# The order of transposed scores and look-ahead scores in the second and third pair of an attention step

## What is computed

```python
x = x + tanh(g_xattn[0]) * xattn(layernorm(x), ctx)
fused = layernorm(x) @ (Wa * col_scale)            # Q, K, V; col_scale from w_std, w_rec
scores = einsum('bhtd,bhsd->bhts', Qf, Kf) / sqrt(D)
scores = where(causal, scores, -max)
attn = softmax(scores); out = attn @ V
x = x + tanh(g_ffn[0]) * (out @ Wp)
```

## Time and profile before

| | |
|---|---|
| median of 3 runs | 578.65 us |
| the profiled execution | 577.93 us |
| its span in the trace | 576.2 us |
| PE busy | 482.2 us, 84% |
| DVE busy | 343.2 us, 60% |
| ACT busy | 262.6 us, 46% |
| POOL busy | 193.2 us, 34% |
| mean granted TensorE clock | 0.953 of full speed |

### The profile page before, as it was taken

How to read it: one execution, slowest core, us unless ns; L and a number is a source line. 1 busy time by engine, 2 the same in 40 slices (tenths; PEclk the granted TensorE clock), 3 DMA queues, 4 the chain that set the end, 5 groups by cost and what they waited for, 6 DMA issues and landing times.

```text
span 576.2 us, 8459 instructions
## 1 busy us (share of the span) xinstructions
PE 482.2 (84%) x2408; PEld 346.9 (60%) x2408; DVE 343.2 (60%) x970; ACT 262.6 (46%) x575; POOL 193.2 (34%) x288
## 2 busy tenths in 40 slices
PE   0036887887998999898798999898798999999977
PEld 0024765555776768665575768665576667666646
DVE  4779647579675353479776235568866116546522
ACT  0856333666544322556554322446565423434540
POOL 4665829137322252126422243124622100212210
PEclk9999999998897999798898999898899899999999
DMA  7202064332400243332400144422300134234001
GB/s 248 117 1 73 4 193 97 97 89 67 118 1 2 61 101 116 120 82 51 132 0 1 41 100 114 128 61 60 84 0 1 28 88 101 66 88 110 20 18 74
DMA packets 28022, 42.55 MB, mean 74 GB/s; under 512 B 8272, under 2 KB 8528, under 8 KB 27984
## 3 DMA queue, kind: packets, MB, share of 16 engines
q1 hardware_dynamic: 26448, 41.97, 26.2%
q10 hardware_dynamic: 1536, 0.14, 0.2%
HBM read 12.59 MB, written 4.19 MB: 29 GB/s over the span
## 4 chain that ended last, share of the span: by engine, by line
PE 57%; DVE 20%; ACT 11%; issue 6%; DMA 2%; ACTq 1%; SPq 1%; POOL 1%; DVEq 0%; POOLq 0%
PE pv_bank L631 10%; PE mm_bank L509 10%; PE mm_bank L510 9%; PE mm_bank L511 9%; ACT work L883 4%; DVE max_bank L1103 4%; PE max_bank L600 4%; PE exp_bank L617 3%; PE mm_bank L661 3%; PE mm_bank L659 3%; PE mm_bank L660 3%; PE turn_bank L517 2%; ACT tile_buf L822 2%; DVE x_amax L1056 2%; DMA col_root<-in_L_ffn_w_rec 1%
## 5 line engine op out<-in xcount | busy, mean ns | idle before, releaser
L1103 DVE CUSTOM_DVE_ANT_0 max_bank<-max_bank,causal 128x512 f32<-128x512 f32 (+3 forms) x256 | 119.1, 516 | 37.3 <-PE max_bank L600 34.5
L406 POOL TENSOR_SCALAR_AFFINE_SELECT work<-work 128x384 f32<-128x384 f32 x64 | 34.2, 534 | 270.0 <-ACT work L883 270.0
L883 ACT ACTIVATE work<-exp_bank 128x512 f32<-128x512 f32 (+1 forms) x192 | 91.1, 523 | 3.2 <-PE exp_bank L617 2.7
L617 PE MATMUL exp_bank<-q_stack,k_stack 97*128 97x512 f32 (+3 forms) x256 | 73.8, 371 | 7.8 <-ACT work L883 4.9
L631 PE MATMUL pv_bank<-work,v_aug 128*33 128x256 f32 (+3 forms) x512 | 75.1, 435 | 0.0
L600 PE MATMUL max_bank<-k_stack,q_stack 96*128 96x512 f32 (+3 forms) x256 | 65.1, 351 | 10.4 <-DVE row_max L1103 8.8
L1086 DVE SCALAR_TENSOR_TENSOR qk_lo<-mm_bank,col_root,qk_hi 128x512 fp32r<-128x512 f32 x32 | 24.0, 750 | 75.6 <-ACT qk_hi L856 75.6
L856 ACT ACTIVATE qk_hi<-mm_bank,col_root 128x512 fp32r<-128x512 f32 x32 | 22.0, 688 | 84.1 <-PE mm_bank L511 84.1
L617 PEld LDWEIGHTS exp_bank<-q_stack,k_stack 97*128 97x128 f32 x256 | 44.7, 197 | 25.2 <-ACT work L883 15.8
L600 PEld LDWEIGHTS max_bank<-k_stack,q_stack 96*128 96x128 f32 x256 | 46.6, 200 | 21.9 <-DVE row_max L1103 12.0
L509 PE MATMUL mm_bank<-xt_hi,w_hi 128*128 128x512 f32 x128 | 57.3, 448 | 2.3 <-DVE xt_lo L1139 1.6
(11 more groups left out here) (138 smaller groups left out, 900.9 us busy)
## 6 DMA issues: line engine op xcount, KB each, us to landing
q_stack<-qk_hi SPq DMA_DIRECT2D x128, 64.0 KB, 2.0
k_stack<-qk_hi SPq DMA_DIRECT2D x128, 64.0 KB, 2.0
x_all<-in_x SPq DMA_DIRECT2D x16, 256.0 KB, 3.9
ctx_raw<-in_ctx SPq DMA_DIRECT2D x16, 256.0 KB, 4.1
q_stack<-qk_lo SPq DMA_DIRECT2D x64, 64.0 KB, 2.0
k_stack<-qk_lo SPq DMA_DIRECT2D x64, 64.0 KB, 2.0
out<-x_all SPq DMA_DIRECT2D x16, 256.0 KB, 2.1
work<-in_L_ffn_Wa SPq DMA_DIRECT2D x3, 768.0 KB, 9.4
```

The lines of the kernel that those rows point to most:

```text
L406: pool.affine_select(out=three, in_=three, compare_op=ALU.is_ge, fill=0.0, base=0, pattern=[[0, 3], [1, P]], channel_multiplier=-1)
L617: last = pe.matmul(bank[:, col:col + T - P * i], k_stack[0:97, s, j, P * i:P * i + P], q_stack[0:97, s, j, P * i:T], start=True, stop=True)
L883: act.activation(prob[j][:, UNIT_COL[k]:UNIT_COL[k] + UNIT_LEN[k]], exp_bank[(3 * j + k) % 2][:, 0:UNIT_LEN[k]], ACT.Exp, scale=SCALE).the ...
L1103: last = dve.tensor_tensor_reduce(max_bank[unit % 2][:, col:col + width], max_bank[unit % 2][:, col:col + width], causal[:, T - width:T], ...
```

## The change

In each of steps 0 to 6, TensorE's second pair of look-ahead units (2 and 3) moves from ahead of gap 1 to behind the second pair of transposed units, and its third pair (4 and 5) moves from ahead of gap 2 to behind the third pair of transposed units, so ahead of gap 3. VectorE's maxima follow: the second pair is now behind gap 1 and `normalise`, the third behind gap 2. The first pair stays where it is. No instruction is added or removed, and ScalarE's, GpSimd's and the DMA queues' orders stay as they are.

```diff
@@ TensorE, body, for u in range(STEPS) @@
                     exp_pair(u, 0)
-                    if ahead:
-                        max_pair(b, u + 1, 1)
                     fill(u, 1)
                     if u:
                         turn_values(b, u - 1)
                     exp_pair(u, 1)
                     if ahead:
-                        max_pair(b, u + 1, 2)
+                        max_pair(b, u + 1, 1)
                     fill(u, 2)
                     exp_pair(u, 2)
+                    if ahead:
+                        max_pair(b, u + 1, 2)
                     fill(u, 3)
@@ VectorE, body, for u in range(STEPS) @@
                     beside(u, 0)
-                    if u + 1 < STEPS:
-                        max_pair(b, u + 1, 1)
                     fill(u, 1)
-                    beside(u, 1)
                     if u:
                         normalise(b, u - 1)
                     if u + 1 < STEPS:
+                        max_pair(b, u + 1, 1)
+                    beside(u, 1)
+                    fill(u, 2)
+                    if u + 1 < STEPS:
                         max_pair(b, u + 1, 2)
-                    for gap in (2, 3):
-                        fill(u, gap)
-                        beside(u, gap)
+                    beside(u, 2)
+                    fill(u, 3)
+                    beside(u, 3)
                 normalise(b, STEPS - 1)
```

## The result

| | before | after |
|---|---|---|
| median, four runs of each in turn | 578.97 us (578.58 to 580.43) | 606.84 us (601.08 to 608.45) |
| ratio | | 1.0459 [1.0386, 1.0531] |
| the profiled execution | 577.93 us | 601.08 us |
| its span | 576.2 us | 599.4 us |
| mean granted clock in it | 0.953 | 0.943 |

The change costs 27.9 us; I had predicted 24.8. The profiled execution is the quickest of the four runs of the new kernel. The other three took 606.1 to 608.5 us, with a granted clock of 0.929 to 0.930. So the trace shows the loss with less of the clock's part in it than the median has.

The account below looks back on a forecast made before the run. The prediction took TensorE's instruction stream to bound the kernel. Later hand-overs, 13.8 + 4.55 = 18.4 us, plus 6.4 us of clock made 24.8 us on 577.93; with 0.7 us for the median, 603.4 us, range 590 to 612.

Parts of the forecast that it names:

- What bounds it: Whole kernel: TensorE's instruction stream sets the time; lateness of the turned maxima costs fully unless a later wait shrinks.
- An unfilled step, +0.85 us: Last sequence, steps 1, 3, 5 with empty gaps: VectorE's 1.25 us for the third pair delays the turned maxima, +0.85 us.
- A filled step, +0.5 us: Last sequence, steps 0, 2, 4, 6: gap 3's work hides the maxima; the pair and its wait stay, +0.5 us.
- The last sequence, +4.55 us: Last sequence: three unfilled steps at 0.85 and four filled at 0.5 us, together +4.55 us.
- Sequences 0 to 2, +13.8 us: First three sequences: step 1 +1.6, steps 0 and 2 +0.6, step 3 -0.3, steps 4 to 6 +0.7 us each; 13.8 together.
- Step 3: Sequences 0 to 2: the one place that can gain, through X1's 2.68 us wait; -0.3 us, ends -2.7 and +0.85.
- The clock, +6.4 us: Four more falls to half clock, step 1 in three sequences and one in the last, 1.6 us each: +6.4 us.
- Two banks are enough: Rival: look-ahead units alternate between two banks, so no hand-over is late; 578.65 us, within 0.2%; chance 0.04.
- faster: Rival: X1's wait goes in full in three sequences, 8 us, other steps at zero; 570.6 us; chance 0.04.
- More falls: Rival: ten falls of the clock, 16 us, on top of the 18.4 us of hand-overs; 613 us; chance 0.1.
- Without the clock: Rival: the same later hand-overs but no clock loss; 597 us, as 590 to 598; chance 0.3.
- What would show it: Profile signs: row_max wait over 20 us, exponentials' near 15.8 or more, turned maxima 2.5 us behind, X1 at most 2.7, clock 0.93.

Follow-up runs that it names:

- the cover: Three pieces of the last sequence moved into empty gaps 3 of steps 1, 3 and 5: on the change 607.0 us, on the kernel before 579.08 us.
- the extra matmuls: The change plus 18 matmuls nobody reads, behind the third look-ahead pair in unfilled steps and step 1: 596.3 us, ratio 1.0322 to its own before.
- the mix: The kernel before with the change's orders in step 3 of sequences 0 to 2 alone, plus the cover's table: 576.71 us against 580.2, ratio 0.9948.

## Why the prediction was right, and where it was off

The predicted 603.4 us, with a range of 590 to 612, stands against 606.84. The mechanism held: TensorE waits for VectorE's last maxima at the end of the step, and the clock adds to it. Point by point:

- **What bounds it.** TensorE's queue behind the turned maxima sets the time. In the unfilled step the third pair brings the whole loss, and a second pair in the change's place costs nothing (1.18 us from the second to the third transposed pair, 1.24 before). Right there. That the second pair's move is free everywhere was wrong: step 5 of the second sequence lost 0.40 us by the third pair and 0.54 by the second.
- **An unfilled step, +0.85 us.** Measured +1.07 (9.11 against 8.04). VectorE's chain was sized well: it ends 2.40 us behind the third transposed pair (540.60 less 538.20), where my times gave 2.35. But I put the turned maxima 0.2 us behind its end, and they stand 0.40 behind it (541.00). The last unit of the next step's first pair can't be written until unit 5 is read out, so its matmuls and the hand-over itself lie there. That was the missing 0.2.
- **A filled step, +0.5 us.** The pair 3+4 gives 1.71 less 1.07, so 0.64, and 0.68 a step with the cover. The upper bound of 0.6 would have been nearer. What was missing is the second pair, which I had put at nothing: step 0 of the last sequence loses 0.36 us by the third pair alone and 0.63 by both.
- **The last sequence, +4.55 us.** At full clock throughout (the change with the extra matmuls) 68.40 less 62.71, so 5.7 us; the two terms above explain the difference.
- **Sequences 0 to 2, +13.8 us.** With the extra matmuls 10.9 us (4.7, 2.9 and 3.4), but with 36 us at half clock in these steps against 45 before. By the price of half clock in the next point I estimate about 15 us at one clock, of which 1.5 are the extra matmuls of step 1. Step by step, where the trace of the change and one before it have full clock: step 0 +0.57 us (first sequence, forecast +0.6), step 4 +0.35 (13.23 against 12.88 in the run of the kernel before with extra matmuls, forecast +0.7), step 5 +0.9 (forecast +0.7). From the first transposed unit to the next step's first look-ahead unit, step 1 of the first sequence loses 1.56 us (6.49 against 4.93, forecast +1.6) and step 2 of the second 0.95 (5.77 against 4.82, forecast +0.6). Step 3 was mis-sized: -1.0, -1.5 and -0.7 us instead of -0.3 each. The last is the cleanest, with 4.3 us at half clock in both kernels. X1's wait did shrink from the 2.68 us of the earlier trace rows:

```profile
286.28 0.66 PE L517 MATMUL turn_bank<-ident,tile_buf 128*128 128x128 f32 x4 [1.45 <-DVE xt_lo L1072]
```

  and VectorE's `xt_lo` waits fell from 9.4 to 5.6 us in all. I had let the later arrival of VectorE from step 2 eat nearly all of it. The sum of the hand-overs still came out right, 18.4 us against 18.8 (596.3 less 577.51). That is partly luck: terms that were too small in the last sequence and in steps 2 and 5 met some that were too large in steps 3 and 4, and the 18.8 has the extra matmuls' own time in it.
- **The clock, +6.4 us.** In the profiled execution it was of the size that I counted. The time at half clock is twice the span times one less the clock: 68 us against 54.6, so 13.7 us more, or four stretches of the 3.4 us that step 6 of the last sequence had (two times 0.16 of 10.63). Its price can be read where two traces show one step with and without it: step 6 of the last sequence (1.56 us for 3.4), step 1 of the second (12.77 us with 3.7 in the kernel before, 11.18 with none), and its step 4 (13.84 with 2.1, 12.88 with none), so 0.43 to 0.46 us for each. By that the 13.7 us cost about 6 of the 23.2 us, and 17 are left for the hand-overs (an estimate from these rows). But the places were right only in part, and there the count was luck. Step 1 of the first sequence and the last sequence each got 3.4 us more, as forecast. Step 1 of the second and third got less than before (1.4 and 1.0 us, against 3.7 and 3.9), and step 2 of all three got 2.4 to 6.1 us where none was before. The three other runs had some 85 us, about nine stretches more than before. The step that was off is thus the number and the place of the falls: I counted them by likeness to one execution, and their number isn't the same from run to run. On the median the clock's part is larger than 6.4 us. The extra matmuls took away 7.7 to 10.5 us, and within the change itself 17 us more at half clock went with 6.3 us (601.08 against 607.4, the mean of the other three).
- **Which rivals fell.** "Two banks are enough" and "faster" are out: the wait of X1 kept 1.45 of its 2.68 us, and no step but step 3 gained at one clock. "More falls" was half right, nine instead of ten in most runs. "Without the clock" is near what the extra matmuls made of the kernel: 596.3, where the rival gave 597.
- **What would show it.** The turned maxima 2.5 us behind the third transposed pair: 2.80. The wait for exponentials near 15.8 or more: 21.6. X1 at or under 2.7: 1.45. The clock near 0.93: 0.943, and 0.93 in the other runs. That sign didn't fit my own sum: four falls more give 0.943, eight or nine give 0.93. The wait for maxima over 20 us: only 17.9 (in the row; in the row of TensorE's matmuls it rose from 8.8 to 16.3). There I had forgotten that the pair's own 0.4 us of matmuls is busy time on the path, not a wait.

My view of the second pair was right only for the change's place and an unfilled step of the last sequence. I took it for free in general; it costs 0.3 to 0.5 us in the filled steps just named, and the run with it ahead of the second transposed pair cost 8%.

**What stays open.** Why one execution has four more falls and another nine isn't settled; nor is which stretch of waits makes the clock fall. In the kernel before, a stretch with 1.4 us of waits in 5.1 stood ahead of a fall. After, so did step 5 of the last sequence with 0.9 us in 9.11, while its unfilled step 3, as long and as idle (8.20 of 9.11 us busy), was followed by none: the step behind it took 9.54 us at full clock. By the Trainium skill, "TensorE: Matmul & The Clock Gate", section "HAM oscillation — how this bites in real kernels", waits between bursts of matmuls cause them. The traces agree that far: the extra matmuls, which filled just such waits, brought the time at half clock from 68 us (85 in the other runs) to 51. Whether the change in step 3 alone gains isn't clear either, and no run gave the look-ahead units a third bank, which would be the direct test of the wait for units 3, 4 and 5.

## What to carry to other kernels

Before moving a producer towards the end of a step, ask what stands behind it in the queue: work is free only in another engine's shadow, and the consumer's time for it (here 1.25 us of VectorE for 0.4 us of TensorE) needs its own cover ahead of whoever needs the result or the bank. Where a move makes TensorE wait more, price the clock too, from several runs and not from one trace, because the number of falls differs from run to run. And waits that can't be removed can be filled with matmuls that nobody reads, but only where the bank is free and the wait would be there anyway.

## What the runs showed of the hardware

- Work that is thrown away can pay. 18 extra matmuls (36 records, 20.1 us busy) took the change from 606.84 to 596.3 us (1.3% by the ratios). 15 of them took the mix from 576.71 to 569.22 us, 2% under the kernel before, and brought the clock from 0.952 to 0.969 in the profiled runs.
- The spread of the runs goes with the granted clock. Of the kernel before, one run took 576.73 us at 0.953 and another 584.96 us at 0.941. The change widened the spread (601.08 to 608.45 us), and its extra matmuls narrowed it again (596.07 to 598.15).
- The clock's effect isn't local. Step 3 of the second sequence took 15.45 us before with 4.7 us of it at half clock, 13.92 in the change with 2.7, and 13.28 with the extra matmuls, which are all in other steps, with none. Part of what looks like the gain of X1's shorter wait is this. In the third sequence the change had 4.3 us at half clock in step 3, as before, and gained 0.7, which is nearer to what the wait alone gives.
